# A layer's two-way convolution, shared out over three engines beside a scan

## The reference, cut to what matters

```python
def _mamba(h, in_proj_W, conv_w, conv_b, x_proj_W, dt_proj_W, dt_proj_b, A_log, Dp, out_proj_W):
    x, z = jnp.split(h @ in_proj_W, 2, axis=-1)          # 512 channels each
    xc = jnp.transpose(x, (0, 2, 1))
    xc = jax.lax.conv_general_dilated(xc, conv_w, (1,), [(D_CONV - 1, 0)], feature_group_count=D_INNER, ...)  # 4 taps
    x = _silu(jnp.transpose(xc, (0, 2, 1)) + conv_b)
    xdbl = x @ x_proj_W
    dt = jax.nn.softplus(xdbl[..., :DT_RANK] @ dt_proj_W + dt_proj_b)
    ...                                                   # scan over 64 positions, 32 states
    return y * _silu(z) @ out_proj_W

fwd = _mamba(h, *mp)
bwd = jnp.flip(_mamba(jnp.flip(h, 1), *mp), 1)
```

## Time and profile before

| | |
|---|---|
| Median of 3 runs | 4603.52 us (4598.18 to 4604.94) |
| The profiled execution's own time | 4607.73 us |
| Its span, first to last instruction | 4605.7 us |
| Busy: PE, DVE, ACT, POOL | 93%, 89%, 87%, 82% |
| Mean granted TensorE clock | 0.983 of 2.4 GHz |
| The eight runs of layer L1 | 324.3 to 1708.3 us from the start |

### The profile page before, as it was taken

The page is one execution under the profiler, slowest core; times in us unless marked ns, Lnnn a source line. Parts: engine busy times, 40 slices in busy tenths (PEclk is TensorE's granted clock), DMA queues, the critical chain, the costliest instruction groups (busy, mean ns, idle before and its releaser), DMA issues.

```text
span 4605.7 us, 81410 instructions
## 1 busy us (share of the span) xinstructions
PE 4305.0 (93%) x31832; PEld 3546.6 (77%) x31832; DVE 4109.4 (89%) x4047; ACT 3986.3 (87%) x6252; POOL 3776.8 (82%) x1219
## 2 busy tenths in 40 slices
PE   7989899999999998999999999999899999999988
PEld 5458788788878884458888888888887888888887
DVE  5659999999999985659999999999998999999996
ACT  3559899799889974559999999999999999999995
POOL 3328788778778883339999999999998999999996
PEclk8999999999999998999999999999999999999999
DMA  4002221111111221022242232322422322323221
GB/s 164 1 17 69 56 60 62 55 58 63 57 53 62 63 84 40 1 39 70 74 85 73 87 68 74 83 68 79 85 68 71 82 79 80 72 77 64 74 78 40
DMA packets 241389, 303.35 MB, mean 66 GB/s; under 512 B 116448, under 2 KB 175712, under 8 KB 241008
## 3 DMA queue, kind: packets, MB, share of 16 engines
q1 hardware_dynamic: 241008, 298.15, 22.9%
HBM read 289.84 MB, written 8.26 MB: 65 GB/s over the span
## 4 chain that ended last, share of the span: by engine, by line
PE 41%; ACT 33%; DVE 14%; issue 6%; POOL 5%; DVEq 0%; DMA 0%; SPq 0%; POOLq 0%; ACTq 0%
PE psum L1081 11%; PE psum L1065 9%; PE psum L807 8%; ACT weights_c L1607 7%; ACT work L1628 7%; DVE work L2065 7%; ACT work L1607 6%; PE psum L1181 5%; ACT weights_c L1628 5%; PE psum L1062 4%; DVE weights_c L2065 3%; POOL work L2451 2%; ACT L1387 2%; POOL weights_c L2451 2%; ACT modulation L1607 1%
## 5 line engine op out<-in xcount | busy, mean ns | idle before, releaser
L2451 POOL TENSOR_TENSOR work<-work,weights_a 128x2048 f32<-128x2048 f32 x512 | 2101.1, 4114 | 272.7 <-DVE work L2065 272.0
L2065 DVE TENSOR_TENSOR_SCAN work<-weights_c,psum 128x512 f32<-128x512 f32 x1316 | 1511.4, 1201 | 83.0 <-PE psum L1065 74.8
L1081 PE MATMUL psum<-ident,work 128*128 128x128 f32 x8192 | 1236.9, 275 | 14.7 <-POOL work L2451 14.4
L2451 POOL TENSOR_TENSOR weights_c<-weights_c,weights_a 128x2048 f32<-128x2048 f32 x256 | 1051.4, 4122 | 15.6 <-DVE weights_c L2065 15.4
L1065 PE MATMUL psum<-ident,work 128*128 128x128 f32 x5464 | 955.9, 278 | 75.0 <-ACT weights_c L1628 32.5
L1081 PEld LDWEIGHTS psum<-ident,work 128*128 128x128 f32 x8192 | 967.0, 142 | 20.7 <-POOL work L2451 20.3
L1065 PEld LDWEIGHTS psum<-ident,work 128*128 128x128 f32 x5464 | 660.9, 142 | 285.2 <-issue 149.8
L1607 ACT ACTIVATE work<-work,decay 128x504 f32<-128x504 f32 x1172 | 821.7, 709 | 35.8 <-DVE weights_c L2065 19.0
L1065 PE MATMUL psum<-ident,weights_c 128*128 128x128 f32 x4432 | 771.6, 275 | 0.0
L2065 DVE TENSOR_TENSOR_SCAN work<-work,psum 128x512 f32<-128x512 f32 x586 | 675.8, 1199 | 26.5 <-PE psum L1065 18.8
L2065 DVE TENSOR_TENSOR_SCAN weights_c<-work,psum 128x512 f32<-128x512 f32 x586 | 676.8, 1199 | 19.6 <-PE psum L1065 16.8
(11 more groups left out here) (204 smaller groups left out, 6240.4 us busy)
## 6 DMA issues: line engine op xcount, KB each, us to landing
weights_a<-c_rows SPq DMA_DIRECT2D x384, 512.0 KB, 3.7
work<-b_diagonals SPq DMA_DIRECT2D x240, 128.0 KB, 3.3
weights_c<-b_diagonals SPq DMA_DIRECT2D x112, 128.0 KB, 2.1
b_diagonals<-weights_c SPq DMA_DIRECT2D x1, 4096.0 KB, 16.2
weights_c<-in_L_cond_fwd_in_w SPq DMA_DIRECT2D x8, 512.0 KB, 5.4
...
```

Source lines behind the costliest of these rows:

```text
L1081: last = nc.tensor.matmul(PS[:, i, k * P:(k + 1) * P], flat[:, at:at + P], IDENT[:, :], start=begins and k == 0, stop=ends and k == DC - 1 ...
L2065: v.tensor_tensor_scan(buf["ring"][s % RING][:, j // 2, along, j % 2], buf["decay"][q % DECAYS[l]][:, along], PS[:, 4 + q % LOOKAHEAD, alo ...
L2451: g.tensor_tensor(state, state, row.unsqueeze(1).unsqueeze(3).broadcast_to([P, 2, T, 2]), ALU.mult).then_inc(ss["prod_ready"], 1)
```

## The change

VectorE no longer adds the last two backward taps. It keeps five full instructions and the short one in a chunk: the tap 0 of both directions now takes the bias along, then come the backward tap 1 (`back{j}_1`) and the forward taps 1 to 3. They stand in the steps read+3 to read+5. In step read+6 ScalarE copies the chunk from PSUM into SBUF (`raw{j}`, which now frees bank 7 for `in{j+1}`), scales the copy by one weight (`near{j}`) and then, in place, by the other (`far{j}`); each of the three waits for the one before. GpSimd adds `near{j}` and `far{j}` to the backward sum, shifted by two and three positions, in the first state whose end is at or behind step read+7 and read+8. `silu_x` is one instruction over four chunks without bias, in all runs. The gap behind `in0` to `in2` goes from 7 to 10 steps. Further waits: ScalarE's taps of chunk 2 and 3 wait for GpSimd's adds of chunk 0 and 1 (two buffers in `TAP1`), and the readers of `XC1` and of the scratch for the last add.

```diff
     if first:
-        jobs += [(f"in{j}", KC, 7) for j in range(DC - 1)] + [("in3", KC, 14 if gated else 12), ("bc", DC, 3)]
+        jobs += [(f"in{j}", KC, 10) for j in range(DC - 1)] + [("in3", KC, 14 if gated else 12), ("bc", DC, 3)]
...
         if first:
-            v += [f"conv{j}_{i}" for j in range(DC) for i in (0, 1, 3, 2, 4, 5, 6, 7)] + ups
-            a += (["silu_g"] if gated else []) + ["silu_x", "bc"]
+            v += [n for j in range(DC) for n in (f"conv{j}_0", f"back{j}_0", f"back{j}_1", f"conv{j}_1", f"conv{j}_2",
+                                                 f"conv{j}_3")] + ups
+            g += [f"back{j}_{k}" for j in range(DC) for k in (2, 3)]
+            taps = [f"{n}{j}" for j in range(DC) for n in ("raw", "near", "far")]
+            before = 12 if r >= 0 else 9
+            a += taps[:before] + (["silu_g"] if gated else []) + ["silu_x"] + taps[before:] + ["bc"]
...
+        TAP1 = region(SCR, 0, 2, 2, T)
...
-                            yield from product(f"in{j}", [by("dve", f"conv{j}_7")], chunk(W1["inp"], j), h,
+                            yield from product(f"in{j}", [by("act", f"raw{j}")], chunk(W1["inp"], j), h,
                                                first(lambda: h_made(r)))
...
-                        for j in range(DC):
-                            last = f(XS1[:, j, :], source[:, j, :], ACT.Silu, bias=vec("L1_cond_conv_b", j))
-                        last.then_inc(done("silu_x"), 1)
+                        f(XS1, source, ACT.Silu).then_inc(done("silu_x"), 1)
                         tables(EXP_LN)
+
+                    def taps(j, later):
+
+                        yield plan.read(f"in{j}", later)
+                        made("dve", f"conv{j}_3@{r}")
+                        if j >= 2:
+                            made("pool", f"back{j - 2}_3@{r}")
+                        far, near = TAP1[:, j % 2, 0, :], TAP1[:, j % 2, 1, :]
+                        f(far, bank[f"in{j}"], ACT.Copy).then_inc(done(f"raw{j}"), 1)
+                        made("act", f"raw{j}@{r}")
+                        at = VCONV + j * 4
+                        f(near, far, ACT.Copy, scale=VEC[:, at + 1:at + 2]).then_inc(done(f"near{j}"), 1)
+                        made("act", f"near{j}@{r}")
+                        f(far, far, ACT.Copy, scale=VEC[:, at:at + 1]).then_inc(done(f"far{j}"), 1)
...
                     if norm1:
+                        for j in range(DC if r >= 0 else DC - 1):
+                            yield from taps(j, 6)
                         yield from silu_x(plan.read("in3", 7), XS1, convolved)
+                        if r < 0:
+                            yield from taps(DC - 1, 6)
...
-                    for shift in range(4):
...
-                            for d in (1, 0) if shift == 1 else (0, 1):
...
+                    v.tensor_scalar(XS1[:, j, :], bank[f"in{j}"], tap(0), bias, ALU.mult,
+                                    ALU.add).then_inc(done(f"conv{j}_0"), 1)
+                    v.tensor_scalar(back[:, :, SEQ - 1:SEQ], x[:, :, SEQ - 1:SEQ], tap(0), bias, ALU.mult,
+                                    ALU.add).then_inc(done(f"back{j}_0"), 1)
+                    yield plan.read(f"in{j}", 4)
+                    made("dve", f"conv{j}_0@{r}")
+                    v.scalar_tensor_tensor(out=back[:, :, 0:SEQ - 1], in0=x[:, :, 1:SEQ], scalar=tap(1),
+                                           in1=ahead[:, :, 0:SEQ - 1], op0=ALU.mult,
+                                           op1=ALU.add).then_inc(done(f"back{j}_1"), 1)
+                    for shift in (1, 2, 3):
+                        yield plan.read(f"in{j}", 4 + shift // 2)
+                        made("dve", f"back{j}_1@{r}" if shift == 1 else f"conv{j}_{shift - 1}@{r}")
+                        inside = ahead[:, :, shift:SEQ]
+                        v.scalar_tensor_tensor(out=inside, in0=x[:, :, 0:SEQ - shift], scalar=tap(shift), in1=inside,
+                                               op0=ALU.mult, op1=ALU.add).then_inc(done(f"conv{j}_{shift}"), 1)
...
-                        ahead("conv0_7", "in1")
+                        ahead("conv0_3", "in1")
...
-                        ahead("conv1_3", "in3")
+                        ahead("conv2_0", "in3")
...
+                    if r % 2 and head:
+                        for j in range(DC):
+                            for shift, scaled in ((2, "near"), (3, "far")):
+                                yield plan.read(f"in{j}", 5 + shift)
+                                made("act", f"{scaled}{j}@{r}")
+                                made("dve", f"back{j}_1@{r}")
+                                if shift == 3:
+                                    made("pool", f"back{j}_2@{r}")
+                                to = by_sequence(XC1[:, j, :])[:, :, 0:SEQ - shift]
+                                of = by_sequence(TAP1[:, j % 2, 3 - shift, :])[:, :, shift:SEQ]
+                                g.tensor_tensor(to, to, of, ALU.add).then_inc(done(f"back{j}_{shift}"), 1)
```

34 lines of the change are left out of this document (13 added, 21 removed).

## The result

The changed kernel takes 4608.5 us (median of 20 runs, 4602.2 to 4614.3) against 4601.2 (20 runs, 4596.5 to 4606.6) on the same chip: ratio 1.0016, interval 1.0010 to 1.0023, so 7.3 us slower. The forecast was 4590, its range 4577 to 4607. The profiled execution took 4603.62 us with a span of 4601.8.

The account below looks back on a forecast made before the run. DVE was taken to pace the convolution stretches, with ACT and POOL having spare time there. Terms -16.8 - 6 + 4 + 6.2 - 1.5 = -14.1 gave 4589.4 from the median 4603.5; forecast 4590 us, range 4577 to 4607.

Parts of the forecast that it names:

- Taps off DVE: Convolutions of runs 1, 3 and 5: eight taps fewer a run at 0.70 us count in full, -16.8 us.
- The hand-over of the bank: Convolutions of runs 1, 3 and 5: half of DVE's 11.5 us idle time goes, -6 us, from 0 to -11.5.
- Behind the stretch: Behind the convolutions, where ACT paces: chunk 3's taps +2.0, merged silu -0.65, three times; +4 us, from 0 to +6.
- The way into run 0: Ahead of run 0's first scan: later squares +0.8, taps before the silu less its merging +5.4; +6.2 us, +5 to +7.
- The even runs: Runs 0, 2, 4 and 6: merged silu gives 0.65 us in run 0, 0.3 in each other; -1.5, from 0 to -2.6.
- Adds on POOL: Convolution stretches: two adds a chunk, about 2.1 us, fit POOL's idle time; nothing, at most +1 us a run.
- rival of blocked scans: Convolution stretches: POOL's 24 adds of 1.05 us each stop DVE's scans, +25 on -14, 4614 us; chance 0.03.
- rival that ScalarE becomes the pace inside the stretch: Convolution stretches: ACT reaches `raw` late, 6 us of taps a run reach the scans; +12, 4615 us; chance 0.10.
- my rivals: Whole kernel: ACT pacing 0.10, blocking adds 0.03, only the taps saved (4600 us) 0.24, all idle time gone (4580) 0.09.
- no wait of TensorE for DVE before `in`: Sign in the convolutions: PE's waits before `in` no longer for DVE and under 1 us.
- the 330 to 331 foretold: Sign at the start of run 0: the first scan at 330 to 331 us in place of 324.3.
- The sign that mattered most: Convolution stretches of runs 1, 3 and 5: shorter by 6 to 10 us each, four taps a chunk.

Follow-up runs that it names:

- x8: The changed kernel once more, unchanged: 4608.5 us against 4601.7 for the kernel before, ratio 1.0014.
- x4: The kernel before once more, unchanged, as the control: 4612.0 us beside 4612.2, ratio 1.0001.
- x5: The kernel before with only the gap behind `in0` to `in2` changed from 7 to 10 steps: 4598.6 us against 4601.7, ratio 0.9996.
- x2: The changed kernel without ScalarE's taps and GpSimd's adds, the last two backward taps left out: 4602.1 us, ratio 0.9979 to the kernel before.
- x1: The changed kernel with the block convolved ahead of run 0 done as before: 4607.4 us against 4612.2 for the kernel before, ratio 0.9991.
- x10: x1 with chunk 3 keeping all six taps on VectorE: 4584.9 us against 4599.2 for the kernel before, ratio 0.9966.
- x11: x1 with ScalarE scaling both taps straight out of the bank, without the copy: 4589.8 us against 4599.2 for the kernel before, ratio 0.9978.
- x7: The changed kernel with ScalarE's taps of chunks 0 to 2 before the first gelu ahead of run 0: 4601.1 us against 4601.7 before, ratio 1.0002.
- x3: The changed kernel with the old gap of 7 steps behind `in0` to `in2`: 4632.5 us, ratio 1.0044 to the kernel before.
- x6: x1 with chunk 3's two scalings behind the silu in runs 1, 3 and 5: 4589.2 us against 4601.7 for the kernel before, ratio 0.9975.
- x9: x6 with four silus in place of the merged one ahead of run 0: 4588.7 us against 4599.2 for the kernel before, ratio 0.9975.

## Why the prediction was wrong

Two steps failed. The work that ScalarE took over was priced by ScalarE's own time, at +4 us behind the convolutions and +6.2 on the way into run 0; it cost +6.8 to +9.5 and +10.2 to +11.7, since TensorE waits behind it and then often runs at 1.2 GHz. And TensorE's wait for the bank was counted as a gain of 6 us when it goes; it gave 2.8 to 5.4, and nothing that the total shows. The even runs, foretold 1.5 us shorter, were 4.0 to 5.1 longer, and most of that stays unexplained.

The ledger, by the prediction's own terms. The second column of measured numbers is x8 less x4. From x4 over x5 and x2 to x8 the runs 1, 3 and 5 change by -2.8, -14.1 and +9.5 us, which adds up to its -7.4.

| term | foretold | first profiles | x4 to x8 |
|---|---|---|---|
| runs 1, 3, 5: taps off DVE, idle time, tail | -18.8 | -10.1 | -7.4 |
| the way into run 0 | +6.2 | +10.2 | +11.7 |
| even runs | -1.5 | +4.0 | +5.1 |
| sum | -14.1 | +4.1 | +9.4 |
| median of the runs | -13.5 | +7.3 | +6.8 |

*Taps off DVE, -16.8:* held in kind. From x5 to x2, which differ in the taps (and in the bias and the merged silu), runs 1, 3 and 5 lose 14.1 us. It is 2.7 less than foretold. DVE's busy time in the three runs falls by 12.9 us from x5 to x2: a tap that depends on the one before is spaced by 0.74 to 0.76 us, where the earlier trace rows had eight in 5.4, and the opening pair takes 0.81 and 0.28 in place of 0.75 and 0.22.

*The hand-over of the bank, -6:* this step failed. TensorE's wait for L1899 in the earlier trace rows did go, but x5 shows what it was worth: 7.1 us of waits, 1.1 us of run 3, 2.8 over the three runs (5.4 against the first profile; the total, -1.8 us with an interval from -6 to +2, doesn't settle it). The same 7.1 us came back as waits for the scan, since DVE set the pace. I had read TensorE's wait as the cause of DVE's idle time. That the saving then did not show in the changed kernel at all is the next term.

*Behind the stretch, +4, from 0 to +6:* mis-sized; it is +9.5 (x8 less x2, runs 1, 3 and 5), or +6.8 from x1, which has the same code in these runs but starts run 0 as before. Not all of it lies behind the stretch: 1.6 us of run 5 stand in the convolution. I had counted ScalarE's 2.0 us for chunk 3 and taken off 0.65 for the merged silu. What I left out is the second link: TensorE waits for the silu 3.6 us in place of 1.6 (x2) or 1.5 (x10), its clock falls to 1.2 GHz, and the scans wait for its inputs. x10 takes away the cause, and the tail of run 3 is 2.9 us shorter. By x11's pair of tails I estimate some 1.2 of the 2.9 for the low clock and the rest for the longer wait.

*The way into run 0, +6.2:* the mechanism held (the nine taps, 6.1 us; squares later by 1.5 in place of 0.8), the size did not: +10.2 and +11.7. The bound of +7 was too tight, for the same reason: this step failed too. After 8.06 us of idle time TensorE ran the 8 `bc` matmuls and the 24 of `down` 3.6 us slower. x7 and x1 show both halves: the place of the taps is worth 5.4 us of way, and 7.3 us in the total; the whole block is worth 11.5 in the total.

*The even runs, -1.5:* wrong in sign, and the term that is off by most, 5.5 to 6.6 us. In run 2 without a slower stretch the state with the silu takes 5.5 us with one merged silu (x3) as with four (x4): TensorE is busy for 5.5 of them. So the merged silu gives nothing there. In run 0 its state takes 6.4 us in x10 in place of 7.1, near the 0.65 foretold, but the run is only 0.2 us shorter. Runs 2, 4 and 6 take either 167.3 or 168.4 to 168.5; the longer ones have one 3.4 us stretch at 1.2 GHz in their fourth state (at 1040.4 us in run 4 of the changed kernel). The changed kernel has it in all three, the kernel before in one and x4 in none. Why it comes in some kernels and not in others I can't say; it was gone from runs 4 and 6 in x6, x9 and x11, and with run 0 as before the even runs take 658.5 to 661.7 us, against 658.6 to 659.7 before. So no part of this loss is shown to belong to the merged silu. Run 0's 158.3 in place of 156.7 came with the old place of the taps only (after, x3, x8).

*Adds on POOL, 0:* right. Each took 1.08 or 1.23 us, and the scans kept their length, 1201 ns in the convolution of run 3 against 1205 in the earlier trace rows:

```profile
L2089 DVE TENSOR_TENSOR_SCAN work<-weights_c,psum 128x512 f32<-128x512 f32 x34 | 39.2, 1201 | 0.0
L2421 POOL TENSOR_TENSOR work<-work,scratch 128x496 f32<-128x496 f32 x4 | 4.3, 1077 | 0.0
```

So the rival of blocked scans is out. The rival that ScalarE becomes the pace inside the stretch is out at spacing 10 and was shown at 7 (x3). None of my rivals was the case: what the experiments could take away of the slower outcome came from the two places where ScalarE's new work stood ahead of a silu for which TensorE waited. I had named both, priced both by ScalarE's own time, and not asked what TensorE does in the wait.

Of what I said would show it: scans of 1.2 us and no wait of TensorE for DVE before `in` came true. The first scan at 329.98 us looks like the 330 to 331 foretold, but that is luck: the way is 10.2 us longer and not 6.2, and all that lies ahead of it came 4.5 us sooner in this execution. The sign that mattered most did not come: the convolutions of runs 1, 3 and 5 were to be 6 to 10 us shorter each, and the whole runs are only 3.9, 4.1 and 2.1 shorter. New and unforeseen, `in0` is asked for at one step for both halves and waits 0.98 us for `h`, and DVE then 1.53 us for it, once a run.
